# Moving the tenth destination one-hot of a sorted group from VectorE to ScalarE in a two-layer graph kernel

## Chip, cores and metric

One core of one Trainium2 chip (trn2) runs the whole program. The metric is the time of one execution on the device, in microseconds (us), as the median of several runs.

## The reference

Two graph layers over 12,500 nodes with 32 features and 400,000 edges, each with a layer norm and a relu ahead of it:

```python
h = jnp.maximum(_layernorm(x, axis=-1), 0.0)
x = x + segment_sum((h * node_vec1)[src], dst) * node_vec1_n2
h = jnp.maximum(_layernorm(x, axis=-1), 0.0)
x = x + (1.0 + eps) * h + segment_sum(relu(h[src] + edge_attr), dst)
```

The edges come sorted by dst; src is random. So each layer gathers 400,000 rows of a node table and adds each to the row of its destination.

## The kernel before

**Units and batches.** An edge unit is 128 partitions by 25 edges, 3,200 edges; there are 125 units, in 25 batches of five. Of a batch, three units are "sorted" and two are "plain". A node table lies in SBUF as `parts`, three bf16 parts of each of the 32 features (96 columns), 100 nodes on each of 125 partitions, and in HBM as `table0` and `table1`.

**Sorted units.** VectorE works out (`rank_within` L1358 and around it, `rank_sums` L1386 to L1396, `rank_places` L1409 to L1427) the place of each edge among those whose source lies in the same bucket of nodes. GpSimd (POOL) then scatters each edge as a record to that place in HBM: 75 indirect DMAs of 128 records each (`scatter`, L709). A record holds a source key and a destination, in layer two the edge's attributes too. SP loads the scattered records back (`load_record`, L550) once all 75 have landed, as 100 tiles of 128 edges, and these are worked on in ten groups of ten tiles. For group g:

- PE turns the source keys into rows (`turn_keys`, L1056), ScalarE copies them to SBUF (`copy_keys`, L820, two copies), and VectorE compares them with the row numbers (`src_onehots`, L1619, two instructions of 1,280 columns);
- PE picks the node rows with these one-hots (`pick`, L1074), ScalarE copies them from PSUM (`copy_candidates`, L828, two copies);
- VectorE makes ten destination one-hots of 224 columns (`dst_onehots`, L1638; the first tile of a batch has 320), by comparing `window_iota` with each edge's destination, and PE multiplies them with the rows (`products`, L1102), adding in PSUM. The one-hots have two buffers, `dst_onehot(g, t)` with g % 2, so group g writes over group g - 2 when its products are done.

**Plain units of layer one** (in all batches but the last). Of the 50 edges on a partition, sorted by source, the outer 30 are picked from SBUF ("direct": `wide_onehots` L1694, `pick_wide` L1159, `copy_wide` L906, `direct_onehots` L1705, `direct_products` L1171), and the 20 in the middle are gathered by POOL with an indirect DMA each (`gather_mid`, L690). Their one-hots are made on ScalarE in two steps: Abs of (destination - iota) (`mid_distances`, L888), then Relu of 1 minus that (`mid_onehots`, L896, 1,120 columns at a time). In the last batch POOL gathers all 50 (`gather`, L697), and VectorE makes their one-hots (`plain_onehots`, L1659).

**Layer two** works in the same batches and groups with other stages between them; there all 50 plain edges are gathered (L697) and ScalarE makes the one-hots of the plain units with the same two steps.

**What sets the order.** Each engine's instructions are written out by hand, in one stream per engine that waits on semaphores. The batches run as 0, 1, a loop over pairs, and the last ones. In a batch of layer one POOL issues the 75 scatters of the next sorted records and then the 20 gathers: `scatter(b)` waits for the ranks of b, for its staged attributes and for the padding; `gather_mid(b)` for the sorted rows of the plain units and for the last middle products. The ranks of batch b + 2 are worked out on VectorE at the end of batch b, and right behind them the first source and destination one-hots of batch b + 1. In the last batch but one there are no more ranks. In the group loop (g from -1 to 9) the order is

- ScalarE: `copy_keys(g+3)`, `copy_candidates(g+2)`;
- PE: `turn_keys(g+3)`, `products(g)`, `pick(g+2)`;
- VectorE: `dst_onehots(g+1)`, `src_onehots(g+3)`.

In `dst_onehots` VectorE pauses: after every third one-hot in layer one (every fifth in layer two) it waits for its own semaphore `dst_paused` before the next, but not after the tenth. In `src_onehots` it waits after each of the two.

## Time and profile before

| | |
|---|---|
| median of 3 runs | 4991.05 us (4982.14 to 4993.16) |
| the profiled execution | 4992.93 us, its span 4991.1 us |
| PE | busy 3947.7 us (79%) |
| PE weight loads | 2974.3 us (60%) |
| VectorE (DVE) | 3814.8 us (76%) |
| ScalarE (ACT) | 2985.4 us (60%) |
| GpSimd (POOL) | 3756.2 us (75%) |

The span is the stretch from the first to the last instruction of the profiled execution. Busy time counts the time in which an engine executes an instruction; issuing, branches and semaphores are not counted, so that an engine with a share of 75% can still have no free time. Layer one reaches to about 3260 us, layer two from about 3300 us to the end.

### The profile page before, as it was taken

How to read it: one execution, taken by the hardware profiler on the slowest of the kernel's cores; microseconds unless marked ns; L12 is line 12 of the kernel's file. 1: busy time of each engine (PE TensorE's matmuls, PEld its weight loads, DVE VectorE, ACT ScalarE, POOL GpSimd, SP SyncE). 2: the span in 40 equal slices, each digit the busy share in tenths (PEclk: the TensorE clock that was granted, in tenths of full speed). 3: DMA queues.
4: the chain of work that ended last, by engine and by line, in shares of the span. 5: the costliest groups of instructions: out<-in, count | busy, mean ns of one | idle time of the engine just before them, and what ended most of it. 6: DMA issues, size and time to landing. Idle time of an engine off the chain costs nothing.

```text
span 4991.1 us, 129116 instructions
## 1 busy us (share of the span) xinstructions
PE 3947.7 (79%) x44428; PEld 2974.3 (60%) x44428; DVE 3814.8 (76%) x11503; ACT 2985.4 (60%) x7899; POOL 3756.2 (75%) x3712
## 2 busy tenths in 40 slices
PE   0688889888888888988888899847777777777775
PEld 0455656666666666666666666636666666666664
DVE  9777878788888888878787888577777777777776
ACT  1456656565656565656566666636666666666664
POOL 6777777777777777777777777747777777777774
PEclk9999999999999999999999999968888888888887
DMA  6222222222222222222222221122222221222221
GB/s 107 53 52 53 53 53 53 53 53 53 53 53 53 53 53 53 53 53 52 53 53 53 53 52 29 31 71 55 56 52 56 55 50 47 52 56 56 56 55 25
DMA packets 437208, 265.05 MB, mean 53 GB/s; under 512 B 330740, under 2 KB 421220, under 8 KB 430120
## 3 DMA queue, kind: packets, MB, share of 16 engines
q1 hardware_dynamic: 318264, 185.91, 16.3%
q0 software_dynamic: 116960, 65.42, 7.5%
q8 instruction: 402, 6.59, 0.6%
q10 hardware_dynamic: 1296, 4.79, 0.3%
q14 instruction: 286, 2.34, 0.2%
HBM read 176.35 MB, written 79.52 MB: 51 GB/s over the span
## 4 chain that ended last, share of the span: by engine, by line
PE 33%; POOL 28%; DVE 20%; issue 14%; ACT 3%; DMA 2%; DVEq 1%; SPq 0%; ACTq 0%; POOLq 0%
PE candidates L1159 21%; POOL stage L697 20%; DVE arena L1638 6%; POOL records L709 6%; PE plain_ps L1171 6%; DVE arena L1619 4%; DVE counts L1386 2%; POOL message L690 2%; PE sorted_agg L1102 1%; PE candidates L1074 1%; ACT arena L820 1%; DVE counts L1394 1%; DVE counts L1389 1%; DMA stage<-in_edge_attr 1%; PE plain_ps L1131 1%
## 5 line engine op out<-in xcount | busy, mean ns | idle before, releaser
L709 POOL DMA_INDIRECT records<-stage,place_i x1875 | 1929.6, 1029 | 593.5 <-issue 570.6
L697 POOL DMA_INDIRECT stage<-table,src_plain x1250 | 1256.7, 1005 | 406.3 <-issue 378.1
L906 ACT ACTIVATE message<-candidates,member_is 128x96 bf16<-128x96 f32 x3600 | 916.6, 352 | 629.8 <-PE candidates L1159 626.8
L1638 DVE TENSOR_SCALAR arena<-window_iota,dst_rel 128x224 bf16<-128x224 f16 (+1 forms) x5000 | 1146.6, 300 | 45.2
L1102 PE MATMUL sorted_agg<-arena 128*96 128x224 bf16 (+1 forms) x5000 | 667.9, 288 | 208.2 <-DVE arena L1638 207.8
L820 ACT ACTIVATE arena<-key_rows 125x640 f16<-125x640 f16 x1000 | 649.1, 707 | 213.4 <-PE key_rows L1056 109.8
L1102 PEld LDWEIGHTS sorted_agg<-arena 128*96 128x96 bf16 x5000 | 550.2, 138 | 238.8 <-DVE arena L1638 237.5
L1619 DVE TENSOR_SCALAR arena<-arena,row_key 125x1280 bf16<-125x1280 f16 x1000 | 566.5, 567 | 136.5 <-ACT arena L820 110.9
L1159 PE MATMUL candidates<-parts,arena 125*128 125x480 bf16 x3072 | 661.8, 366 | 0.0
L690 POOL DMA_INDIRECT message<-table,mid_src x480 | 507.5, 1057 | 146.4 <-issue 143.3
L1056 PE MATMUL key_rows<-ident,record 128*125 128x128 f16 x5000 | 417.4, 233 | 203.8 <-DMA record<-records 114.2
L1082 PE MATMUL candidates<-record,ident 128*128 128x320 f32 x500 | 237.8, 563 | 404.4 <-DVE arena L1619 404.1
L1056 PEld LDWEIGHTS key_rows<-ident,record 128*125 128x125 f16 x5000 | 377.4, 148 | 239.8 <-issue 138.7
L1159 PE MATMUL candidates<-parts,xs 125*128 125x480 bf16 x2280 | 506.3, 368 | 0.0
L1171 PE MATMUL plain_ps<-summed,message 128*96 128x224 bf16 x3600 | 482.1, 271 | 0.0
L1087 PEld LDWEIGHTS candidates<-parts,arena 125*128 125x128 bf16 x15000 | 427.4, 99 | 90.3 <-issue 75.5
L1171 PEld LDWEIGHTS plain_ps<-summed,message 128*96 128x96 bf16 x3600 | 406.5, 130 | 120.9 <-issue 8.2
L1159 PE MATMUL candidates<-parts,record 125*128 125x480 bf16 x1992 | 474.6, 369 | 4.1 <-DVE record L1694 4.0
L828 ACT ACTIVATE arena<-candidates 128x480 bf16<-128x480 f32 x500 | 262.1, 569 | 353.2 <-PE candidates L1074 348.7
L1159 PEld LDWEIGHTS candidates<-parts,arena 125*128 125x128 bf16 x3072 | 298.5, 98 | 278.4 <-issue 4.1
L1087 PE MATMUL candidates<-parts,arena 125*128 125x32 bf16 x15000 | 427.2, 180 | 4.6 <-issue 4.6
L1694 DVE TENSOR_SCALAR arena<-direct_row,wide_key 125x640 bf16<-125x640 f16 x672 | 233.5, 389 | 239.1 <-PE candidates L1159 228.8
(222 smaller groups left out, 5053.0 us busy)
## 6 DMA issues: line engine op xcount, KB each, us to landing
record<-records SPq DMA_DIRECT2D x50, 1650.0 KB, 7.5
stage<-in_edge_attr SPq DMA_DIRECT2D x125, 400.0 KB
records<-pad SPq DMA_DIRECT2D x25, 1650.0 KB
records<-stage,place_i POOLq DMA_INDIRECT x1875, 2.2
stage<-table,src_plain POOLq DMA_INDIRECT x1250
message<-table,mid_src POOLq DMA_INDIRECT x480
xs<-in_x SPq DMA_DIRECT2D x8, 390.6 KB
table<-parts ACTq DMA_DIRECT2D x4, 585.9 KB
```

The source lines that it names most:

```text
L690: pool.indirect_dma_start(mid_message[:, j, :], None, table0, bass.IndirectOffsetOnAxis(ap=mid_src[:, h, j:j + 1], axis=0)).then_inc(gathe ...
L697: pool.indirect_dma_start(message[:, k, j, :] if l == 0 else rows[:, k, j, :], None, table0 if l == 0 else table1, bass.IndirectOffsetOnAx ...
L709: pool.indirect_dma_start(records, bass.IndirectOffsetOnAxis(ap=place_i[:, h, e:e + 1], axis=0), stage[:, h, e, :], None).then_inc(scatter ...
L820: nc.scalar.activation(key_row[:, g % 2, k * HALF * P:(k + 1) * HALF * P], key_rows[k][0:NP, 0:HALF * P], ACT.Copy).then_inc(key_rows_copi ...
L906: last = nc.scalar.activation(direct_message[n % DB][:, m * WIDE:(m + 1) * WIDE], candidates[n % 2][:, m * WIDE:(m + 1) * WIDE], ACT.Copy, ...
L1056: last = nc.tensor.transpose(key_rows[k][0:NP, t * P:(t + 1) * P], column, ident16[:])
L1087: last = nc.tensor.matmul(candidates[g % 2][:, tile * F:(tile + 1) * F], src_onehot[:, g % 2, o, tile * P:(tile + 1) * P], parts[:, 2 * bu ...
L1102: last = nc.tensor.matmul(into, sorted_message[:, (2 * h + g) % MESSAGES, t, :], dst_onehot(g, t), start=(g == 0 and t == 0), stop=(g == G ...
L1159: last = nc.tensor.matmul(candidates[n % 2][:, 0:MEMBERS * WIDE], wide_onehot(s, w)[:, i * P:(i + 1) * P], parts[:, w * MEMBERS:(w + 1) * ...
L1171: last = nc.tensor.matmul(pair_agg, direct_message[n % DB][:, m * WIDE:(m + 1) * WIDE], direct_onehot[:, n % DO, :], start=(n == 0 and m = ...
L1619: nc.vector.tensor_scalar(src_onehot[:, g % 2, o, :], key_row[:, g % 2, :], row_key[0:NP, o:o + 1], None, ALU.is_equal).then_inc(src_oneho ...
L1638: last = nc.vector.tensor_scalar(dst_onehot(g, t), window_iota[:, 0:WA if tile == 0 else WT], dst_rel[:, h, tile:tile + 1], None, ALU.is_e ...
```

## The change

In layer one's sorted groups 2 to 9 VectorE makes nine one-hots, and ScalarE the tenth: an Abs of (destination - iota) over 224 columns into the buffer of the one-hot, and one group later a Relu of 1 minus that, in place. In ScalarE's group loop the Relu of group g + 1 stands behind the key copies and the Abs of group g + 2 behind the candidate copies. PE's products wait for one semaphore more. VectorE's pauses are now after the third and the sixth one-hot in these groups; the former one after the ninth is not there, as the ninth is the last.

```diff
+                def tile_distances(b, h, g):
+
+                    act.wait_ge(dst_rel_ready[0], b + 1)
+                    act.wait_ge(sorted_done[0], GROUPS * b + g - 1)
+                    tile = g * GROUP + GROUP - 1
+                    nc.scalar.activation(dst_onehot(g, GROUP - 1), window_iota[:, 0:WT], ACT.Abs,
+                                         bias=dst_rel[:, h, tile:tile + 1], scale=-1.0).then_inc(distances_ready, 1)
+
+                def tile_onehot(b, g):
+                    act.wait_ge(distances_ready, (GROUPS - 2) * b + g - 1)
+                    nc.scalar.activation(dst_onehot(g, GROUP - 1), dst_onehot(g, GROUP - 1), ACT.Relu,
+                                         bias=one[:, 0:1], scale=-1.0).then_inc(tile_onehot_ready, 1)
...
                     def group(g):
                         if g + 3 < GROUPS:
                             copy_keys(b, h, u, g + 3)
+                        if g >= 1 and g + 1 < GROUPS:
+                            tile_onehot(b, g + 1)
                         if g in (7, 8) and not is_last(b):
                             copy_direct_keys(b, g - 7)
                         if g + 2 < GROUPS:
                             copy_candidates(b, h, u, g + 2)
+                        if g >= 0 and g + 2 < GROUPS:
+                            tile_distances(b, h, g + 2)
...
-                    act.wait_ge(distances_ready, 2 * b + k + 1)
+                    act.wait_ge(distances_ready, (GROUPS - 2) * BATCHES + 2 * b + k + 1)
...
                     pe.wait_ge(dst_onehot_ready[l], nth + 1)
+                    if l == 0 and g >= 2:
+                        pe.wait_ge(tile_onehot_ready, (GROUPS - 2) * b + g - 1)
...
-                    for t in range(GROUP):
+
+                    tiles = GROUP - 1 if l == 0 and g >= 2 else GROUP
+                    paused = nth * ((GROUP - 1) // run)
+                    if l == 0:
+                        paused = (6 + 2 * (GROUPS - 2)) * b + (3 * g if g < 2 else 6 + 2 * (g - 2))
+                    for t in range(tiles):
...
-                        if t % run == run - 1 and t < GROUP - 1:
+                        if t % run == run - 1 and t < tiles - 1:
                             last.then_inc(dst_paused[l], 1)
-                            dve.wait_ge(dst_paused[l], nth * ((GROUP - 1) // run) + t // run + 1)
+                            dve.wait_ge(dst_paused[l], paused + t // run + 1)
```

## Rows read from the trace of the kernel before

**Rows 1.** The page's chain that ended last, by engine and by line.
```profile
PE 33%; POOL 28%; DVE 20%; issue 14%; ACT 3%; DMA 2%; DVEq 1%; SPq 0%; ACTq 0%; POOLq 0%
PE candidates L1159 21%; POOL stage L697 20%; DVE arena L1638 6%; POOL records L709 6%; PE plain_ps L1171 6%; DVE arena L1619 4%; DVE counts L1386 2%; POOL message L690 2%; PE sorted_agg L1102 1%; PE candidates L1074 1%; ACT arena L820 1%; DVE counts L1394 1%; DVE counts L1389 1%; DMA stage<-in_edge_attr 1%; PE plain_ps L1131 1%
```

**Rows 2.** Busy time by engine from 171.0 to 3184.6 us; last row of a longer answer.
```profile
core 0: us, PE busy (x) PEld busy (x) DVE busy (x) ACT busy (x) POOL busy (x), PEclk, DMA share, GB/s
...
171.00:3184.60 3013.60, 2673.49 (x21763) 1836.74 (x21760) 2390.05 (x7168) 1813.47 (x5295) 2325.18 (x2260) 0.96 0.25 50
```

**Rows 3.** POOL's waits, 171.0 to 3184.6: us in total, times, longest us.
```profile
POOL records L709 <- issue: 548.0, 1799, 0.3
POOL message L690 <- issue: 137.2, 450, 0.3
POOL message L690 <- DVE key L1427: 3.0, 10, 0.3
```

**Rows 4.** Timeline where the last batch begins: start, length, engine, instructions, idle time before.
```profile
3183.62 0.96 POOL L709 DMA_INDIRECT records<-stage,place_i  x1 [0.30 <-issue]
...
3185.99 0.33 SPq L550 DMA_DIRECT2D record<-records  x1
...
3194.63 0.65 PEld L1056 LDWEIGHTS key_rows<-ident,record 128*125 128x125 f16 x10 [0.51 <-DMA record<-records]
...
3197.12 1.14 DVE L1619 TENSOR_SCALAR arena<-arena,row_key 125x1280 bf16<-125x1280 f16 x2 [19.70 <-ACT arena L820]
```

**Rows 5.** Timeline of one sorted group in the middle of layer one.
```profile
1828.34 1.30 DVE L1619 TENSOR_SCALAR arena<-arena,row_key 125x1280 bf16<-125x1280 f16 x2
...
1828.46 0.93 PEld L1102 LDWEIGHTS sorted_agg<-arena 128*96 128x96 bf16 x10 [1.05 <-DVE arena L1638]
...
1829.67 2.54 DVE L1638 TENSOR_SCALAR arena<-window_iota,dst_rel 128x224 bf16<-128x224 f16 x10
...
1830.39 1.03 ACT L828 ACTIVATE arena<-candidates 128x480 bf16<-128x480 f32 x2 [1.54 <-PE candidates L1074]
...
1831.31 1.31 ACT L820 ACTIVATE arena<-key_rows 125x640 f16<-125x640 f16 x2
1832.14 1.30 DVE L1619 TENSOR_SCALAR arena<-arena,row_key 125x1280 bf16<-125x1280 f16 x2
```

**Rows 6.** Timeline of VectorE, single instructions at the end of a group, last batch.
```profile
3229.47 0.27 DVE L1638 TENSOR_SCALAR arena<-window_iota,dst_rel 128x224 bf16<-128x224 f16 x1
3229.77 0.51 DVE L1638 TENSOR_SCALAR arena<-window_iota,dst_rel 128x224 bf16<-128x224 f16 x1
...
3229.96 0.65 DVE L1619 TENSOR_SCALAR arena<-arena,row_key 125x1280 bf16<-125x1280 f16 x1
```

**Rows 7.** ScalarE's groups from 1854 to 1900 us: count, busy us, mean ns, idle before.
```profile
L888 ACT ACTIVATE centered<-window_iota,pair_dst 128x224 bf16<-128x224 f16 x20 | 8.9, 519 | 0.0
L896 ACT ACTIVATE centered<-centered,one 128x1120 bf16<-128x1120 bf16 x4 | 5.0, 1255 | 0.0
```

**Rows 8.** Timeline of the first changed group in the last batch.
```profile
3216.56 1.03 ACT L828 ACTIVATE arena<-candidates 128x480 bf16<-128x480 f32 x2 [1.67 <-PE candidates L1074]
...
3217.48 1.31 ACT L820 ACTIVATE arena<-key_rows 125x640 f16<-125x640 f16 x2
...
3218.82 1.14 DVE L1619 TENSOR_SCALAR arena<-arena,row_key 125x1280 bf16<-125x1280 f16 x2
```

**Rows 9.** The chain in order of time, at the end of layer one.
```profile
3254.95 1.61 PE plain_ps L1123 x25
...
3303.76 0.96 POOL stage L697
```

**Rows 10.** POOL's groups in 1828 to 1851, 1698 to 1721 and 3910 to 3990 us.
```profile
L709 POOL DMA_INDIRECT records<-stage,place_i x19 | 18.3, 963 | 5.8 <-issue 5.8
L709 POOL DMA_INDIRECT records<-stage,place_i x19 | 18.8, 990 | 5.8 <-issue 5.8
L697 POOL DMA_INDIRECT stage<-table,src_plain x61 | 62.0, 1016 | 18.6 <-issue 18.3 <-DMA stage<-in_edge_attr 0.3
```

More of the change, by code:

```diff
@@ L411, in gnn_two_layers @@
         mid_distances_ready = sem("mid_distances_ready")
+        tile_onehot_ready = sem("tile_onehot_ready")
         direct_done = sem("direct_done")
```

## The prediction

> **What bounds the kernel now.** The first view to read is the chain that ended last. It names PE in front (33%), then POOL (28%), then DVE (20%), and inside DVE the very line that the change shortens, L1638, with 6% of the span [rows 1]. Read alone, it says that a shorter L1638 pays. But the chain only follows one of several streams that run side by side, and at an end where two are nearly level it picks one. So the second view is the busy time in the stretch in which layer one is steady, from 171.0 us (POOL's second scatter) to 3184.6 us (the end of its last). There POOL is busy 2325.2 of 3013.6 us, in 2260 instructions [rows 2]. The third view says what POOL did in the rest: it waited 548.0 us for "issue" before scatters and 137.2 us before gathers, never more than 0.3 us at a time, and 3.0 us more behind a VectorE instruction, again 0.3 us each [rows 3]. 2325.2 + 548.0 + 137.2 + 3.0 = 3013.4 us, the whole stretch. The 0.3 us stand before every indirect DMA, so POOL never waited for any engine: for 24 batches it issued one indirect DMA after the other, 75 scatters and 20 gathers a batch, one each 3013.6/2260 = 1.33 us, 126.7 us a batch.
>
> That such a stream sets the time takes one more step: somebody must wait for it. The fourth view is the timeline where the last batch takes over. The last scatter starts at 3183.62, SP issues the load of the sorted records at 3185.99, and PE's first transposes of that record start at 3194.63, after a wait of 0.51 us for that DMA; VectorE, which has no ranks to work out for later batches here, has then been idle for 19.70 us [rows 4]. Before that batch VectorE and PE were later than the record by nothing that matters; they can't be earlier than it. Whatever VectorE saves in the first 24 batches ends in a longer wait at this place, unless POOL's own stream gets shorter.
>
> **Inside a sorted group** the picture is the other one. Each group starts two source one-hots on VectorE at 1828.34 and the next at 1832.14: 3.80 us, with the ten destination one-hots from 1829.67 between them and no idle time noted. PE waits 1.05 us for L1638, and ScalarE idles 1.54 us before its two copies of candidates, then copies keys from 1831.31 [rows 5]. So in the sorted stage VectorE is the slowest of the three, and only there.
>
> **The change, part by part.**
>
> *VectorE loses the tenth one-hot and a pause.* In eight groups of a batch (g 2 to 9) nine tiles are made in place of ten, and the pause after the ninth falls away, because nothing follows it in the group. In the last batch the ninth starts at 3229.47, the tenth at 3229.77 and the source one-hot at 3229.96 [rows 6]. A follower without a pause comes 0.19 us behind (3229.96 - 3229.77), so after the change the source one-hot could start at 3229.66: 0.30 us saved in a group, 2.4 us in a batch. In batches 0 to 23 I cost this at nothing; the cover is POOL's stream [rows 2, 3], and if that cover were gone the same 2.4 us would be worth 24 x 2.4 = 57.6 us.
>
> *ScalarE gains an Abs and a Relu of 128x224 in those groups.* The Abs has its twin in L888: 20 of them took 8.9 us, 0.445 us each. For the Relu of 224 columns the nearest row is one of 1120 columns, 5.0/4 = 1.25 us, so it lies between 0.25 us (a fifth) and the Abs's 0.445; I take 0.45 [rows 7]. ScalarE's group holds 1.03 us of candidate copies and 1.31 us of key copies [rows 8], 2.34 us; with 0.90 more it is 3.24 us, against a group that shrinks from 3.80 to 3.50. It still fits, with some 0.26 us left. Its new waits are light. The Abs waits until products(g-2) are through; PE runs these ahead of the pick whose candidates ScalarE has just copied, so they are done. The Relu is issued one group after its Abs. Queued behind them are the candidate copies and the key copies; a key copy is needed by VectorE's source one-hot a whole group later. PE's one new wait (tile_onehot_ready, ahead of products(g)) has the Relu a group ahead of it. No DMA is added or moved, SP's queue is not touched, and POOL gets no new wait. Layer two sees only another number in a semaphore wait: nothing.
>
> *The last batch is where VectorE's time is on the path.* After the hand-over its sorted groups run VectorE against itself, and from there the chain goes on over the plain one-hots to PE's L1123 at 3254.95 and to POOL's first gather of layer two at 3303.76 [rows 9], one for one. Of the eight groups the first doesn't pay: the source one-hot at 3218.82 starts when the key copies that began at 3217.48 are through, and those came right behind the candidates of 3216.56 [rows 8]; the new Abs goes in between and delays them by 0.45 us. The other seven pay 0.30 us each. 7 x 0.30 - 0.45 = 1.65 us faster.
>
> *POOL's stream against a denser VectorE.* This is the unknown term, as every nanosecond on POOL's instruction counts in full. A scatter's mean is 963 ns in one batch's sorted stage, the one read above, and 990 ns in another's; 1016 ns is a gather's mean in layer two, where VectorE makes five one-hots between pauses [rows 10]. So POOL is held up a little by what VectorE does, and by how it falls. With the change the third run in a group is three destination one-hots and a source one-hot without a pause between them, in place of one and one; that goes toward layer two's pattern. It touches some 8 x 3.5/1.27 = 22 POOL instructions of a batch, 528 in 24 batches. Ends: all at 963, where now half are at 990, gives -13.5 ns x 528 = -7 us; all at layer two's 1016 gives, from 963, +28 us. The nearest row is layer one's own 990: all at that would be +7 us, all as now 0; I take the middle, +3.6 us.
>
> As to a rule here: the rows just named have VectorE's one-hots and POOL's indirect DMAs nearly indifferent to each other in the sorted stage. The Trainium skill, SBUF — State Buffer, "Who interferes with whom", says that VectorE and GpSimd share a pair of ports under an exclusive lock, and that a tensor_scalar in a two-port mode blocks the other fully. By that each one-hot that leaves VectorE would free POOL for its whole length, and the sum would not end at +3.6 but far below zero; the rivals have it as a case of its own.
>
> **The sum.** The profiled execution took 4992.93 us (span 4991.1), 1.9 us over the median of 4991.05. 4992.93 - 1.65 + 3.6 = 4994.9 us; against the median 4991.05 - 1.65 + 3.6 = 4993.0 us. About 0.2% (10 us) is what a measurement of this kernel can tell from no change, so this is "no change". By the bounds of the stall term it goes from 4982 to 5017.
>
> **Rivals.**
> 1. *VectorE decides after all* (faster). If POOL's stream gave way as VectorE gets ahead, each batch would be 2.4 us shorter: 4991.05 - 57.6 - 1.65 = 4931.8 us. For it: the chain's DVE share [rows 1] and PE's waits in the group [rows 5]. Against it: POOL's account without a gap [rows 2, 3]. 6%.
> 2. *POOL is freed* (faster). As a mechanism of this kernel: each of the 8 x 24 one-hots that go would have held POOL up for the 0.19 us between two starts [rows 6], 36.5 us, so 4991.05 - 36.5 - 1.65 = 4952.9 us. Against it: 963 ns beside a VectorE without idle time; there is nothing like 0.19 us to give back. 5%. It is the lock rule of the page named above.
> 3. *POOL stalls more* (slower). The place is the run of three destination one-hots and a source one-hot at the end of each changed group; the price at layer two's mean is (1016 - 963) ns x 528 = 28 us, so 4991.05 + 28 - 1.65 = 5017.4 us. It decides once the mean in those groups rises by more than (10 + 1.65)/528 = 22 ns. For it: 1016 and 990 against 963 [rows 10]. Against it: run by run three one-hots are still fewer than layer two's five. 15%.
> 4. *ScalarE gets late* (slower). With 0.26 us left in a group, a Relu or a wait that costs 0.5 us more would make ScalarE the group's bound at 3.75 us. In a batch that is still no more than now, so it needs over 0.8 us in each group to pass POOL's pace: 4991.05 + 24 x 8 x 0.1 = 5010 us if the group came to 3.90. 3%.
> 5. *The change does nothing of what it says*, for instance since the tenth one-hot was never what the next waited for: 4991 us. 1%.
>
> **How the numbers follow.** The forecast has 70%. Within 0.2%: the forecast and rival 5, 0.71. Faster: rivals 1 and 2, 0.11. Slower: rivals 3 and 4, 0.18. The range starts at the low bound of the stall term, 4982, and goes up into rival 3 as far as 5010, which takes in about half of it and rival 4; left out are both fast rivals and the worst of the stalls, some 0.2.
>
> **What would show it.** Right: POOL's busy time and 0.3 us waits again fill the stretch from its second scatter to its last, at 1.33 us an instruction; VectorE's groups shrink to 3.5 us or less, yet batches stay at 126.7 us; PE's or VectorE's wait for the record ahead of a batch grows by what was saved; ScalarE's share rises by 200 x 0.9 = 180 us; the last batch's groups are 0.3 us shorter. POOL gaps over 0.3 us, or batches of 124.3 us, would prove it wrong on the fast side; scatters in the sorted stage at a mean over 985 to 990 ns, on the slow side; key copies that VectorE waits for in the middle of the sorted stage would show ScalarE as the bound.

## The result, and the profile after

The changed kernel took 5000.47 us in the median of nine runs (4994.75 to 5009.63), the kernel before 4991.66 us in nine runs on the same chip: a ratio of 1.0023 with an interval of 1.0013 to 1.0032. Forecast were 4993.0 us and "no change". So the time lies in the range, but the change is a small loss, at the edge of what was called no change, and on the side of rival 3. The profiled execution took 5000.13 us, its span is 4998.3 us, 7.2 us more than the one before.

The page of the changed kernel, its busy times and its chain that ended last by engine and by line:

```profile
PE 3917.0 (78%) x44428; PEld 2947.8 (59%) x44428; DVE 3735.4 (75%) x11303; ACT 3121.8 (62%) x8299; POOL 3768.0 (75%) x3712
...
POOL 65%; issue 22%; DVE 6%; PE 3%; DMA 2%; ACT 1%; DVEq 0%; POOLq 0%; SPq 0%; ACTq 0%
POOL records L710 35%; POOL stage L698 21%; POOL message L691 9%; DVE arena L1663 1%; PE candidates L1179 1%; DMA stage<-in_edge_attr 1%; DVE arena L1639 1%; DMA stage<-table,src_plain 1%; PE sorted_agg L1122 1%; ACT centered L974 0%; PE candidates L1105 0%; DMA record<-records 0%; PE candidates L1100 0%; DVE counts L1383 0%; DVE stage L1822 0%
```

VectorE is busy 79 us less, ScalarE 136 us more, POOL 12 us more. In the chain POOL went from 28% to 65% and PE from 33% to 3% [rows 1]. POOL's own work is almost the same: the chain before ran over two streams that were nearly level, and with VectorE ahead it follows POOL alone.

The same stretch as in [rows 2], from POOL's second scatter to the end of its last, as the windows view gives it (the columns are those of that group), and then POOL's waits in it, as in [rows 3]:

```profile
171.00:3201.60 3030.60, 2655.86 (x21801) 1824.33 (x21800) 2318.43 (x6975) 1950.93 (x5692) 2341.90 (x2260) 0.96 0.25 50
```

```profile
POOL records L710 <- issue: 548.1, 1798, 0.3
POOL message L691 <- issue: 140.2, 460, 0.3
POOL records L710 <- DVEq L1625: 0.6, 2, 0.3
```

2341.9 + 548.1 + 140.2 + 0.6 = 3030.8 of 3030.6 us. POOL's stream is again full, with the same 2260 instructions and the same 0.3 us before each, and it is 17.0 us longer, 16.7 of them busy time: its instructions themselves took longer.

The timeline where the last batch begins, as in [rows 4]:

```profile
3200.60 0.96 POOL L710 DMA_INDIRECT records<-stage,place_i  x1 [0.30 <-issue]
...
3202.96 0.33 SPq L551 DMA_DIRECT2D record<-records  x1
...
3210.26 1.14 PEld L1074 LDWEIGHTS key_rows<-ident,record 128*125 128x125 f16 x10 [6.37 <-DMA record<-records]
3210.26 1.32 PE L1074 MATMUL key_rows<-ident,record 128*125 128x128 f16 x10 [5.90 <-DMA record<-records]
...
3212.42 1.32 DVE L1639 TENSOR_SCALAR arena<-arena,row_key 125x1280 bf16<-125x1280 f16 x2 [25.23 <-ACT arena L821]
...
3217.12 1.14 DVE L1639 TENSOR_SCALAR arena<-arena,row_key 125x1280 bf16<-125x1280 f16 x2 [3.38 <-ACT arena L821]
```

The weight load's wait for the record grew from 0.51 to 6.37 us and VectorE's idle time from 19.70 to 25.23 us: here VectorE's saving went. The waits by line say the same of all batches. In the kernel before, PE's waits in its stretch:

```profile
PE sorted_agg L1102 <- DVE arena L1638: 197.5, 174, 2.5
...
PE key_rows L1056 <- DMA record<-records: 22.0, 4, 10.2
```

In the changed kernel, in its stretch:

```profile
PE sorted_agg L1122 <- DVE arena L1663: 106.2, 123, 2.0
PE key_rows L1074 <- DMA record<-records: 101.4, 17, 14.4
...
PE sorted_agg L1122 <- ACT arena L910: 33.5, 16, 2.3
```

PE's matmuls wait 91 us less for VectorE's destination one-hots, and 79 us more for the record that POOL scattered.

So the span's +7.2 us are these: +17.0 of POOL's stream (last scatter ends at 3201.6 in place of 3184.6); -1.7 from there to the first source one-hot of the last batch; -1.64 in the last batch (3212.42 to POOL's first gather of layer two at 3317.42, against 3197.12 to 3303.76); -6.5 in all that follows, layer two, in which the change moves nothing. There the two executions differ by themselves: the shortest and the median gather of layer two took 940 and 944 ns in this one, 943 and 947 ns in the one before. The same 3 ns stand in layer one, where the shortest scatter took 954 ns in this one and 957 before. Over 2260 instructions that is an estimated 6.8 us, so that at an equal pace the stream grew by some 24 us and not by 17.0. Every other trace of this study on chips of 4.99 ms has 954 and 940 ns; compare them with each other first, and with the trace before only with these 6.8 us in mind. At which pace the other timed executions ran no trace shows.

### The profile page after: what moved, and what is told of

Read it like the earlier page. It is cut to its first block, busy times and chain, and to the rows that moved or that the text cites. A ratio compares the mean times of both kernels' runs of the same rounds, so it can differ in the third digit from the quotient of the medians.

```text
span 4998.3 us, 129736 instructions
## 1 busy us (share of the span) xinstructions
PE 3917.0 (78%) x44428; PEld 2947.8 (59%) x44428; DVE 3735.4 (75%) x11303; ACT 3121.8 (62%) x8299; POOL 3768.0 (75%) x3712
## 4 chain that ended last, share of the span: by engine, by line
POOL 65%; issue 22%; DVE 6%; PE 3%; DMA 2%; ACT 1%; DVEq 0%; POOLq 0%; SPq 0%; ACTq 0%
POOL records L710 35%; POOL stage L698 21%; POOL message L691 9%; DVE arena L1663 1%; PE candidates L1179 1%; DMA stage<-in_edge_attr 1%; DVE arena L1639 1%; DMA stage<-table,src_plain 1%; PE sorted_agg L1122 1%; ACT centered L974 0%; PE candidates L1105 0%; DMA record<-records 0%; PE candidates L1100 0%; DVE counts L1383 0%; DVE stage L1822 0%
## 5 line engine op out<-in xcount | busy, mean ns | idle before, releaser
L710 POOL DMA_INDIRECT records<-stage,place_i x1875 | 1962.0, 1046 | 593.9 <-issue 570.7
L1663 DVE TENSOR_SCALAR arena<-window_iota,dst_rel 128x224 bf16<-128x224 f16 (+1 forms) x4800 | 1083.8, 301 | 38.1
L1122 PE MATMUL sorted_agg<-arena 128*96 128x224 bf16 (+1 forms) x5000 | 647.1, 283 | 162.9 <-DVE arena L1663 117.4
L1074 PE MATMUL key_rows<-ident,record 128*125 128x128 f16 x5000 | 431.2, 237 | 327.6 <-DMA record<-records 202.7
L1122 PEld LDWEIGHTS sorted_agg<-arena 128*96 128x96 bf16 x5000 | 536.9, 136 | 187.5 <-issue 119.3
L691 POOL DMA_INDIRECT message<-table,mid_src x480 | 491.7, 1024 | 146.3 <-issue 146.3
L1179 PE MATMUL candidates<-parts,xs 125*128 125x480 bf16 x2280 | 520.6, 376 | 0.0
L1191 PE MATMUL plain_ps<-summed,message 128*96 128x224 bf16 x3600 | 465.1, 264 | 0.0
L1191 PEld LDWEIGHTS plain_ps<-summed,message 128*96 128x96 bf16 x3600 | 389.2, 126 | 121.3 <-issue 8.4
L974 ACT ACTIVATE centered<-window_iota,plain_key 128x128 bf16<-128x128 f16 x1250 | 379.9, 391 | 14.2 <-DVE plain_key L1702 14.2
```

Source lines behind the costliest of these rows:

```text
L691: pool.indirect_dma_start(mid_message[:, j, :], None, table0, bass.IndirectOffsetOnAxis(ap=mid_src[:, h, j:j + 1], axis=0)).then_inc(gathe ...
L710: pool.indirect_dma_start(records, bass.IndirectOffsetOnAxis(ap=place_i[:, h, e:e + 1], axis=0), stage[:, h, e, :], None).then_inc(scatter ...
L1074: last = nc.tensor.transpose(key_rows[k][0:NP, t * P:(t + 1) * P], column, ident16[:])
L1122: last = nc.tensor.matmul(into, sorted_message[:, (2 * h + g) % MESSAGES, t, :], dst_onehot(g, t), start=(g == 0 and t == 0), stop=(g == G ...
L1179: last = nc.tensor.matmul(candidates[n % 2][:, 0:MEMBERS * WIDE], wide_onehot(s, w)[:, i * P:(i + 1) * P], parts[:, w * MEMBERS:(w + 1) * ...
L1191: last = nc.tensor.matmul(pair_agg, direct_message[n % DB][:, m * WIDE:(m + 1) * WIDE], direct_onehot[:, n % DO, :], start=(n == 0 and m = ...
```

## The experiments

Two theories stood against each other for the 17 us that POOL's stream got longer. **A**: the longer run of one-hots without a pause (three destination one-hots and the source one-hot, rival 3) holds up the POOL instruction beside it, group by group. **B**: the shorter group changes the beat in which VectorE's one-hots meet POOL's instructions, whatever is between them. Beside them stood the question whether POOL's stream is the bound at all, and what ScalarE's part costs.

### On a chip where the kernel before takes 8.73 ms

The first four kernels fell on a chip on which every one of them, the kernel before too, takes 1.75 times as long. They can be compared with each other only.

**The change once more** (no edit).

> The change itself, beside the kernels of this call on one chip. Theory (POOL's stream sets layer one, and VectorE's new rhythm stalls POOL's indirect DMAs): again 1.001 to 1.003 of the kernel before, and in most batches one scatter in about three groups' halves (one per two groups, 6.7 us) takes 1.24 us in place of 0.96. Rival (the difference was chance between chips): 0.999 to 1.001.

8701.47 us (5 runs) against 8732.63 (16 runs): 0.9966, 0.9952 to 0.9979. (A ratio is always to the kernel before on the same chip, with its interval behind it.) The change pays here, where 1.001 to 1.003 was expected. Two rows of its trace tell why it is another machine, by the lines view from 2000 to 2040 us (busy us, mean ns, then idle time before and its cause):

```profile
L1092 PE MATMUL candidates<-parts,arena 125*128 125x96 bf16 x8 | 1.9, 237 | 20.5 <-issue 20.5
L1074 PE MATMUL key_rows<-ident,record 128*125 128x128 f16 x7 | 1.9, 264 | 17.8 <-issue 17.8
```

PE stands 20.5 us before eight matmuls and waits for nothing that the profile shows, 2.6 us before each. And its chain that ended last:

```profile
issue 34%; PE 30%; DVE 17%; another core or an unknown queue 15%; ACT 4%; DVEq 1%; POOL 0%; ACTq 0%; POOLq 0%
```

POOL has no share. On this chip issue time, PE and VectorE make up most of the chain, so POOL's stream isn't the bound, which is rival 1's case, and a thinner VectorE pays. Why the issue time is there no run shows.

**The pause after the ninth one-hot put back.**

```diff
@@ dst_onehots, behind the group's nine
+                    if l == 0 and g >= 2:
+                        dve.wait_ge(dst_onehot_ready[0], nth + 1)
```

> The change, and VectorE pauses after the ninth one-hot too, so that no run of three destination one-hots and a source one-hot stands without a pause. Theory A (the long run is what holds POOL up, as the prediction's third rival has it): scatters in the sorted stage go back to a mean under 975 ns, and the time to 4991 - 1.65 = 4989 us, 0.9997 of before. Theory B (POOL is held up by where a source one-hot of 0.55 us falls against its own 1.27 us beat, whatever the run before it): the mean stays over 1000 ns in many batches, or changes with the new beat without a link to the run, and the time stays at 4996 to 5004 us.

8737.08 us (11 runs): 1.0004, 0.9995 to 1.0013. The whole gain of this chip is gone with the pause, which costs 36 us; what the missing tenth one-hot saves by itself is eaten up by ScalarE's part (26 us, below). Of theory A it says nothing, since POOL isn't the bound; the profile has POOL's gathers wait for the sorted rows up to 87 us at a time:

```profile
POOL message L691 <- DVEq L1625: 1967.7, 23, 87.2
```

**No tenth one-hot, no tenth product.**

```diff
-                        if g >= 1 and g + 1 < GROUPS:
-                            tile_onehot(b, g + 1)
-                        if g >= 0 and g + 2 < GROUPS:
-                            tile_distances(b, h, g + 2)
...
-                    for t in range(GROUP):
+                    tiles = GROUP - 1 if l == 0 and g >= 2 else GROUP
+                    for t in range(tiles):
```

> The change without ScalarE's part: the tenth one-hot of groups 2 to 9 in layer one is made by nobody, and PE leaves out the tenth product. VectorE's stream is that of the change. Theory (VectorE's rhythm costs the time): like the change, 5000 us give or take 3. Rival (ScalarE's Abs and Relu, or PE's new wait, cost it): 4989 us.

8662.77 us (5 runs): 0.9918, 0.9905 to 0.9932. Without ScalarE's two instructions and PE's product the gain is 70 us in place of 31.

**ScalarE's part alone**: VectorE makes all ten, ScalarE writes its Abs and Relu into spare room, which PE waits for as in the change.

```diff
-                    nc.scalar.activation(dst_onehot(g, GROUP - 1), window_iota[:, 0:WT], ACT.Abs,
+                    nc.scalar.activation(spare[:, g % 2, :], window_iota[:, 0:WT], ACT.Abs,
...
-                    tiles = GROUP - 1 if l == 0 and g >= 2 else GROUP
+                    tiles = GROUP
```

> ScalarE makes its Abs and Relu as in the change, but into room that nobody reads; VectorE makes all ten one-hots with the pauses of before. Theory (VectorE's rhythm costs the time): as before, 4991 + 0.45 = 4992 us give or take 3. Rival (ScalarE's work costs it): 5000 us.

8759.05 us (6 runs): 1.0032, 1.0019 to 1.0044, a loss of 26 us. On this chip every pause or instruction that was added cost time and every one left out paid, whichever engine had it.

### On chips where the kernel before takes 4.99 ms

**No tenth one-hot, no tenth product**, the kernel above once more.

> Again, on another chip if one is had: the change without ScalarE's part (the tenth one-hot of groups 2 to 9 in layer one is made by nobody, and PE leaves out the tenth product). VectorE's stream is that of the change. Theory (VectorE's rhythm holds POOL up, and POOL's stream sets layer one): like the change, 1.001 to 1.003 of before, and scatters in the sorted stage with a mean over 1000 ns. Rival (ScalarE's Abs and Relu, or PE's new wait, cost the time): 0.9996. Where POOL's stream does not set the pace, as on the chip of the first runs: under 0.995.

4997.84 us (12 runs) against 4989.31 (23 runs): 1.0019, 1.0008 to 1.0029. Nothing of the tenth one-hot's work is left on ScalarE or PE, and by the ratios the kernel is as much slower as the change is (1.0019 against 1.0023, each on its own chip). ScalarE's part costs nothing that can be measured, and the loss comes from what VectorE does with nine.

**One gather more in each batch**, in the kernel before, into a spare tile.

```diff
+                pool.indirect_dma_start(
+                    spare[:], None, table0,
+                    bass.IndirectOffsetOnAxis(ap=mid_src[:, h, 0:1], axis=0)).then_inc(gathered[0][0], 16)
```

> The kernel before, with one indirect DMA more among the 20 gathers of each of 24 batches, into room that nobody reads. Theory (POOL's stream sets layer one): 24 x 1.27 to 1.33 = 30 to 32 us longer, 1.006. Rival (VectorE or PE set it): within 2 us of before.

5010.03 us (10 runs): 1.0039, 1.0027 to 1.0051, so 20.7 us for 24 instructions beside which no other engine got work. The windows view of its stretch:

```profile
171.00:3209.90 3038.90, 2672.76 (x21798) 1832.72 (x21796) 2403.85 (x7167) 1814.68 (x5310) 2342.89 (x2284) 0.96 0.25 50
```

2284 instructions in place of 2260, and a last scatter 25.3 us later than before. 24 x 1.27 would be 30.5 us. In the trace nothing is missing: this execution has the pace of 954 ns, so the 6.8 us come on top, and 25.3 + 6.8 = 32.1 us is 24 x 1.34, an estimate. The time of 20.7 us is less than the 30 to 32 us expected, and why stays open. It is ten times what the rival allowed, so POOL's stream sets layer one here, if not for every microsecond.

**The pause put back**, the kernel above once more.

> Again, on another chip: the change, and VectorE pauses after the ninth one-hot too, so that no run of three destination one-hots and a source one-hot stands without a pause. Theory A (the long run holds POOL up, the prediction's third rival): scatters in the sorted stage back to a mean under 975 ns, and 0.9997 of before. Theory B (POOL is held up where a source one-hot of 0.55 us falls against its own beat of 1.27 us, whatever the run before it): the mean over 1000 ns in many batches, or another beat by luck, and 1.001 to 1.003.

4985.05 us (11 runs) against 4991.15 (27 runs): 0.9991, 0.9982 to 1.0000. It is the fastest kernel on these chips: 15 us under the change (16 by the ratios, as the change ran on another chip), and under the kernel before by 6 us, at the edge of its interval. Its stretch:

```profile
171.00:3183.50 3012.50, 2682.60 (x21806) 1836.87 (x21804) 2351.38 (x6976) 1953.18 (x5693) 2323.78 (x2260) 0.96 0.25 50
```

The stall is gone: POOL's busy time is 2323.8 us, against 2325.2 in [rows 2] and 2341.9 in the change. The traces of this kernel and of the change have the same pace, and the stretch is 18.1 us shorter, all of it POOL's busy time. So far this is what theory A expected, and not the 1.001 to 1.003 of B, which had allowed for it only as "another beat by luck". The next kernel decides between them.

**Ten one-hots on VectorE, without a pause after the ninth**: the run of the change, made longer by one, with the kernel before's work.

```diff
-                        if t % run == run - 1 and t < GROUP - 1:
+                        if t % run == run - 1 and t < (GROUP - 2 if l == 0 and g >= 2 else GROUP - 1):
```

> The kernel before with all ten one-hots on VectorE, but without the pause after the ninth in groups 2 to 9, so that a run of four destination one-hots and a source one-hot stands without a pause, one longer than the change has. Theory A (the run): at least as slow as the change, 1.002 or more. Theory B (the beat): groups still come to about 3.8 us, three of POOL's steps, scatters stay at a mean under 985 ns, and the time within 0.1% of before.

4992.46 us (11 runs): 1.0002, 0.9993 to 1.0011. Here the run at the end of a group is four destination one-hots and the source one-hot, longer than in the change, and the time shows no loss, where A expected 1.002 or more. The trace shows a part of one: its stretch up to the last scatter is 3021.6 us, 8.0 more than before and 9.0 less than the change. But it doesn't lie beside the one-hots. Counting the POOL instructions that are over 0.15 us too long and have a source one-hot at their middle, up to the last scatter, I find 19 in this kernel, 12 in the kernel before, 13 in the one with the pause, and 63 in the change, 63 without the tenth one-hot. What POOL lost here lies for the most part beside the additions to the ranks (L1386 of the kernel before), 25.1 us against 17.5. **Theory A falls**: a longer run beside the same one-hots doesn't bring the change's stalls. B expected groups held at 3.8 us, which is a miss, they are 3.4 to 3.65 us; but here they don't repeat with POOL's step.

**The beat itself**, all engines in the sorted stage of one batch of the change (of the answer the rows of VectorE's source one-hots and POOL):

```profile
2341.17 1.13 DVE L1639 TENSOR_SCALAR arena<-arena,row_key 125x1280 bf16<-125x1280 f16 x2
...
2341.29 1.25 POOL L710 DMA_INDIRECT records<-stage,place_i  x1 [0.31 <-issue]
...
2342.84 0.96 POOL L710 DMA_INDIRECT records<-stage,place_i  x1 [0.30 <-issue]
...
2344.11 1.02 POOL L710 DMA_INDIRECT records<-stage,place_i  x1 [0.30 <-issue]
...
2344.47 1.13 DVE L1639 TENSOR_SCALAR arena<-arena,row_key 125x1280 bf16<-125x1280 f16 x2
...
2345.43 0.99 POOL L710 DMA_INDIRECT records<-stage,place_i  x1 [0.30 <-issue]
...
2346.73 0.96 POOL L710 DMA_INDIRECT records<-stage,place_i  x1 [0.31 <-issue]
...
2347.99 1.25 POOL L710 DMA_INDIRECT records<-stage,place_i  x1 [0.30 <-issue]
```

Two groups start their source one-hots at 2341.17 and 2344.47, and the third does at 2347.87; POOL's instructions of 1.25 us start at 2341.29 and 2347.99. Two groups are 6.70 us, and so are five POOL steps of which one is 0.29 us too long (and two by 0.03 and 0.06). Each time the long one is that which began 0.12 us behind the pair of source one-hots. The second of the pair, by itself in the timeline:

```profile
2341.74 0.55 DVE L1639 TENSOR_SCALAR arena<-arena,row_key 125x1280 bf16<-125x1280 f16 x1
```

It starts 0.45 us into POOL's instruction, and its end at 2342.29 is followed 0.25 us later by POOL's, at 2342.54. The two streams are locked at five to two, so the stall comes back every 6.7 us while this lasts. Up to the last scatter the change has 63 such stalls, three to five in most batches and none or one in seven of the 24.

The same stage with the pause put back, VectorE:

```profile
2337.21 1.30 DVE L1639 TENSOR_SCALAR arena<-arena,row_key 125x1280 bf16<-125x1280 f16 x2 [0.23 <-DVE arena L1663]
2338.55 2.21 DVE L1663 TENSOR_SCALAR arena<-window_iota,dst_rel 128x224 bf16<-128x224 f16 x9
2340.99 1.30 DVE L1639 TENSOR_SCALAR arena<-arena,row_key 125x1280 bf16<-125x1280 f16 x2 [0.23 <-DVE arena L1663]
```

and POOL:

```profile
2337.26 0.96 POOL L710 DMA_INDIRECT records<-stage,place_i  x1 [0.30 <-issue]
2338.52 0.95 POOL L710 DMA_INDIRECT records<-stage,place_i  x1 [0.30 <-issue]
2339.78 0.96 POOL L710 DMA_INDIRECT records<-stage,place_i  x1 [0.30 <-issue]
2341.05 0.96 POOL L710 DMA_INDIRECT records<-stage,place_i  x1 [0.31 <-issue]
```

A group is 3.78 us and three undisturbed POOL steps are 3.79. Now it is VectorE that yields: its pair takes 1.30 us in place of 1.13. The nine one-hots save nothing there (3.80 us in [rows 5]), and that costs nothing, since VectorE isn't the bound. Only a part of this kernel's groups stand at 3.8 us; many take 3.4 to 3.7 us and are free of the stall as well. So what the pause does is to leave the beat of five to two; a lock at three isn't needed for it. Of the four kernels, POOL's lines in 20 us of the same stage, from 2341 to 2361 us and for the last from 2334 to 2354 (count, busy us, mean ns, idle). The change:

```profile
L710 POOL DMA_INDIRECT records<-stage,place_i x15 | 15.5, 1037 | 4.6 <-issue 4.6
```

No tenth one-hot at all:

```profile
L710 POOL DMA_INDIRECT records<-stage,place_i x16 | 16.5, 1034 | 4.9 <-issue 4.9
```

Ten one-hots without the pause:

```profile
L709 POOL DMA_INDIRECT records<-stage,place_i x16 | 15.6, 973 | 4.9 <-issue 4.9
```

The change with the pause put back:

```profile
L710 POOL DMA_INDIRECT records<-stage,place_i x17 | 16.3, 962 | 5.2 <-issue 5.2
```

The two with the loss stand at 1034 and 1037 ns, the two without at 962 and 973. It isn't so in every batch: in one of the change's own, at 1064 us, where the groups came to 3.17 us, which is two and a half POOL steps, the mean was 968 ns. Over all scatters of the 24 batches that have a source or destination one-hot at their middle, the means are 1006 and 1008 ns with the loss, 975 (the kernel before), 971 (the pause) and 975 (ten without it) otherwise. Taking the kernel before's shortest instruction (957 ns for a scatter, 943 for a gather) from each POOL instruction up to the last scatter, and putting the rest down to the VectorE instruction at its middle, I find 15.2 us more beside source one-hots in the change than before (24.2 against 9.0 us), of a total of 17.0 more (185.8 against 168.8). The remainder is a balance of others: 6.9 us more beside the additions to the ranks, 2.5 less beside the scans, and smaller ones.

**A pause after each wide source one-hot of the plain stage**, in the change. It aims at the other places where POOL is held up.

```diff
-    PAIR = 2
+    PAIR = 1
```

> The change, with a pause of VectorE after each of the one-hots for the wide picks and for the direct products (lines 1719 and 1730) in place of after every second. If POOL's stream sets layer one, what frees POOL there pays: stalls of about 0.1 us on each of some 450 indirect DMAs could halve, 25 us, 0.995 of the change. If a pause of 0.035 us is too short for POOL to get in, or PE's picks wait for the later one-hots: 1.000 to 1.005 of before.

4990.65 us (10 runs): 0.9996, 0.9984 to 1.0008, some 10 us under the change. That is less than the 25 us hoped for, and in the range of the other expectation. The stalls beside the wide one-hots fell from 50.8 us, in the kernel before and in the change, to 40.2 us, and the stall beside the sorted source one-hots stayed (25.8 us). POOL now waits now and then, up to 2.1 us at a time. Its stretch:

```profile
171.00:3186.80 3015.80, 2654.43 (x21758) 1828.77 (x21757) 2469.30 (x6976) 1946.73 (x5677) 2321.11 (x2260) 0.96 0.25 50
```

**The ranks cut smaller**, in the change: the scans in quarters in place of halves, and the additions and products by halves.

```diff
-                    for some in (slice(0, BUCKETS * J // 2), slice(BUCKETS * J // 2, BUCKETS * J)):
+                    for some in QUARTERS:
...
-                step(nc.vector.tensor_tensor(counts[:], counts[:], in_bucket[:], ALU.mult))
+                for v in range(SORTED):
+                    step(nc.vector.tensor_tensor(counts[:, v, :], counts[:, v, :], in_bucket[:, v, :], ALU.mult))
```

> The change, with the longest VectorE instructions of the ranks cut: scans of 625 columns into 300 and 325, the adds of 1250 into two of 625, the product of 3750 into three of 1250. VectorE gets 11 + 3 + 2 instructions more in each of 23 batches, which it can afford by the 2.4 us that the change took from it. Theory (POOL's stream sets layer one, and its stalls are what VectorE's instruction in front of it has left): the stalls beside these lines, about 90 us in the change, fall by 35 to 50, and the time to 4950 to 4965 us, faster than both kernels. Rival (VectorE or PE set it): 5000 us or more, as VectorE only gets longer.

5017.08 us (5 runs): 1.0050, 1.0037 to 1.0064. A miss, and slower than the change too: shorter VectorE instructions were to hold POOL up less, and held it up more. The scans of the change, and then of this kernel:

```profile
L1383 DVE TENSOR_TENSOR_SCAN counts<-not_first,in_bucket 128x625 f16<-128x625 f16 x138 | 201.6, 1461 | 4.8
```

```profile
L1384 DVE TENSOR_TENSOR_SCAN counts<-not_first,in_bucket 128x300 f16<-128x300 f16 (+1 forms) x276 | 223.6, 810 | 9.6
```

Twice as many of them, a little over half as long, and POOL's stalls beside scans went from 39.9 us in the change (42.4 in the kernel before) to 58.4 us, over nearly the same number of POOL instructions, 129 and 138. The other parts of the edit did otherwise: beside the additions, also twice as many and half as long, the stalls are about the same (24.4 and 25.7 us), and beside the product and the addition behind it they fell from 26.2 to 20.3 us. So length alone doesn't set a stall, nor does the number of instructions; what does is left open.

**Both pauses together, and the wide one in the kernel before.** These two ran on the chip of 8.73 ms again.

```diff
-    PAIR = 2
+    PAIR = 1
...
+                    if l == 0 and g >= 2:
+                        dve.wait_ge(dst_onehot_ready[0], nth + 1)
```

> The change with the pause after the ninth one-hot and with a pause after each one-hot for the wide picks and the direct products. If POOL's stalls of the two places add: the pause after the ninth took the change to 0.9991 of before, the other pauses brought it from 1.0023 to 0.9996; together 0.997 (the last scatter near 3170 us in the trace). If VectorE and PE are by then as slow as POOL, which the trace of the wide pauses hints at with first waits of POOL of 1 to 2 us: 0.998 to 1.001, and POOL waits for VectorE before scatters.

> The kernel before, with a pause after each one-hot for the wide picks and the direct products. POOL's stalls beside them fall by some 12 us, as they did in the change. Theory (in the kernel before VectorE and PE are level with POOL, so that what VectorE gets more shows at once, and the change's one-hots pay only together with shorter stalls): 0.999 to 1.001, with POOL waiting for the ranks. Rival (POOL's stream alone sets the pace here too): 0.9975.

8833.85 us (4 runs) against 8726.64 (7 runs), 1.0124, 1.0107 to 1.0141, and 8819.26 us (4 runs), 1.0105, 1.0088 to 1.0122. On this chip the pauses only cost: both together 132 us against the change, the wide one 93 us against the kernel before. Whether the two gains add up where POOL is the bound stays open.

## Why the prediction was right in part and wrong in part

- **What bounds layer one** was right. POOL's account is full before, after and in the kernel with the pause; 24 gathers more cost 20.7 us; and what VectorE gained, some 0.45 us a group, ended in longer waits for the record. Rivals 1 and 2 are out on these chips. On the other chip POOL is not the bound, and the change gains 0.34%.
- **ScalarE costs nothing** was right: leaving its part out altogether leaves the time where it is (4997.84 against 5000.47 us, 1.0019 against 1.0023). Its busy time grew by 136 us, less than the 180 us expected. That PE waits for L910 33.5 us in all costs nothing either, for what follows waits for POOL.
- **The last batch's -1.65 us** came as -1.64, but by luck, out of terms that were each off. The timelines have five source one-hots one behind the other: 3231.81, 3235.12, 3238.51, 3241.81, 3245.20 in the change, 3214.99, 3218.82, 3222.44, 3226.20, 3229.96 before. Four groups save 14.97 - 13.39 = 1.58 us, 0.395 us each and not 0.30, and the first of them pays too (3.83 to 3.31 us), where 0.45 us were to be lost. What follows, with the other four groups in it, gives 1.58 again. Against that stand 1.79 us at the start of the batch, which the prediction hadn't seen: between the first two pairs of source one-hots lie 4.70 us in place of 2.91. There PE had waited 5.9 us for the record, and its second ten transposes start 4.12 us behind the first in place of 2.65. The windows view of that place, with the granted clock as third figure from the end, of the change:

```profile
3210.20:3212.00 1.80, 1.74 (x12) 1.43 (x13) 0.00 (x0) 0.91 (x2) 1.19 (x3) 0.50 0.11 14
3212.00:3214.20 2.20, 2.20 (x9) 0.87 (x8) 1.28 (x2) 0.39 (x1) 1.77 (x2) 0.70 0.14 26
```

and before:

```profile
3194.60:3196.50 1.90, 1.87 (x17) 1.24 (x18) 0.00 (x0) 1.87 (x7) 1.29 (x3) 1.00 0.07 13
3196.50:3198.00 1.50, 1.50 (x16) 1.08 (x15) 0.84 (x2) 1.11 (x4) 1.20 (x2) 1.00 0.21 30
```

  The clock fell while PE stood, and after a wait of 5.9 us PE works at 0.50, the lower of its two levels (1.2 GHz), for its first 3.1 us; the 0.70 of the second row is 0.50 up to 3213.3 us and 1.00 behind it. Before, with next to no wait, it works at 1.00 (2.4 GHz). Its ten transposes take 1.32 us in place of 0.79. At the same place the kernels without the tenth one-hot (a wait of 6.7 us) and with the pause put back (6.0 us) fell to the lower level too, and ten one-hots without a pause (2.7 us) did not. So VectorE's gain ahead of the record is not merely useless: the idle time that it makes on PE costs something behind it. What is left is 1.79 - 1.58 - 1.58 - 0.27 (the stretch between) = -1.64 us.
- **POOL's stream, the term that failed.** The step was "the nearest row is layer one's own 990 ... I take the middle, +3.6 us". It measured +17.0 us, over 528 instructions some 32 ns each, where rival 3 decides from 22. The middle of 963 and 990 [rows 10] was right for the kernel before, whose mean over all batches is 975 ns; what had no ground was to take the change as lying between the same two rows. It came to 1006 ns, past the 985 to 990 that the prediction itself named as the sign of being wrong on the slow side. The question to ask of the rows was what beat each has, and what beat the change would set: 3.80 us is three POOL steps, 3.35 us is not, and two groups of it are five steps and a stall. That the time still fell within the range is in part luck: the range reached far into rival 3, and the time moved by 8.8 us, half of what POOL's stream did.
- **Rival 3** was right in its sign and wrong in its mechanism. Its price of 28 us is counted from 963 ns, though the term itself has half the scatters at 990; from 975 ns layer two's 1016 would give (1016 - 975) ns x 528 = 22 us, nearer to the 17.0. The place is not the longer run at the end of the group, since a longer one without the loss exists. It is the second source one-hot, met by POOL's instruction in every second group where the streams are locked.
- **The rule of the lock.** A POOL instruction of 1.25 us that ends 0.25 us behind the end of a 0.55 us source one-hot, and in the kernel with the pause VectorE giving way (1.30 for 1.13 us), are in kind what the Trainium skill, SBUF — State Buffer, "Who interferes with whom", would have: VectorE and GpSimd share a pair of ports, and whichever issues first holds it while the other waits. In size it doesn't fit what these runs show: nine destination one-hots, 2.2 us of nearly gapless VectorE work in each group, pass beside POOL instructions of 0.96 us. If each of them blocked POOL for its length, the tenth one-hot's going would have made POOL faster; it made it slower. No run shows whether these one-hots use both ports.

That POOL's stalls beside the source one-hots are the cause rests on four kernels that stand on either side of them (63 and 63 long instructions with the loss, 19 and 13 without), on a pause that takes 18.1 us off POOL's stream, and on the kernel without ScalarE's part, which has the loss. That it is the beat that brings them is read from the timelines, behind the runs; no kernel set another beat on purpose to test it, for instance by pauses of other lengths. What is not settled: why the streams fall into just this phase and hold it, why some batches find another, why the kernel with the pause is faster than the one before, and which part of POOL's instruction it is that has to wait.

## What to carry to other kernels

Before work is taken off an engine, find the stream that is occupied without a gap; here it had a busy share of 75% and issue time in the rest, and the thinner engine could only wait longer for it. When such a stream bounds, the moments at which the neighbour's instructions fall can count for more than their load: one added pause on an engine with time to spare, worth nothing in any sum of costs, took 15 us off the changed kernel. Before two traces are set against each other for some microseconds, compare the shortest instruction of a kind in each: 3 ns in 957 were worth 6.8 us here. And a resource whose mean differs from batch to batch (963 and 990 ns) has patterns behind it that have to be looked at one by one before any mean is used.

## What the runs showed of the hardware

- VectorE and POOL can fall into step, for several groups on end: three POOL instructions to one group at 3.78 us, five to two at 6.70 us. Either can lose: POOL in one (1.25 for 0.96 us), VectorE in the other (1.30 for 1.13 us).
- Cutting the scans from 1.46 to 0.81 us raised POOL's stalls beside them by half, 39.9 us in the change to 58.4 us; cutting the additions in the same way left theirs at 24.4 and 25.7 us.
- The same indirect DMAs took 3 ns longer throughout in one execution than in the others: 957 in place of 954 ns at the shortest for a scatter, 943 in place of 940 for a gather.
- One chip runs these kernels 1.75 times slower, with 2 to 3 us of unexplained time before single matmuls, and it turns three verdicts round: the change gains there, its pause costs 36 us there, and leaving the tenth out gains 0.8%. A change of some tenths of a per cent is a statement about the chip too.
- A wait of 5.9 us on PE was followed by 3.1 us at the lower clock, where waits of 0.5 and 2.7 us were followed by the full one.
